# Two broadcast rows by DMA through DRAM, and the subtraction of q's maximum on GpSimd, in a fused attention and graph kernel

## What is computed

```python
# layer 0, per batch: x (C=256, N=512)
q, k = wq @ x, wk @ x
scores = leaky_relu(q[None, :] + k[:, None], 0.01)      # N x N
att = softmax(scores, axis=-1)
out0 = relu(adj @ (x @ att.T) + bm[:, None])
h = layernorm(x + out0)
# layer 1, per batch: h (N=256, D=512)
z_l, z_g, v = h @ W_lang.T, h @ W_grav.T, h @ W_V.T
zn = z_l / max(norm(z_l), 1e-8)
A_l = max(zn @ zn.T, 0) * not_eye * mask                # mask = adj
A_g = exp(-dist2(z_g) / (2 sigma^2)) * not_eye * mask
K = w * A_l / rowsum(A_l) + (1 - w) * A_g / rowsum(A_g)
y = layernorm(h + (K @ v) @ W_O.T)
```

## Time and profile before

| | us |
|---|---|
| median of 3 runs | 1203.2 |
| lowest, highest | 1196.25, 1203.94 |
| the profiled execution, its span | 1203.0 |

### The profile page before, as it was taken

How to read it: one execution, slowest core, us unless ns; L and a number is a source line. 1 busy time by engine, 2 the same in 40 slices (tenths; PEclk the granted TensorE clock), 3 DMA queues, 4 the chain that set the end, 5 groups by cost and what they waited for, 6 DMA issues and landing times.

```text
span 1203.0 us, 21861 instructions
## 1 busy us (share of the span) xinstructions
PE 1080.8 (90%) x7296; PEld 712.7 (59%) x7296; DVE 946.9 (79%) x2678; ACT 657.9 (55%) x1299; POOL 333.8 (28%) x316
## 2 busy tenths in 40 slices
PE   7757989989998999999899998989989998998996
PEld 4344756756575675657567565656756565575663
DVE  4557878978787897878789787878978787897867
ACT  2435656565565656556565655656565564756431
POOL 0231414224051422405142240414233041423200
PEclk9979999999999998999999999999999999999998
DMA  7002002020020202002020200102020020201000
GB/s 262 0 1 71 1 1 106 2 105 0 19 85 0 105 0 105 0 21 84 0 105 0 105 0 30 75 0 105 0 105 0 34 71 0 105 0 70 1 35 36
DMA packets 22763, 55.40 MB, mean 46 GB/s; under 512 B 1744, under 2 KB 2256, under 8 KB 20688
## 3 DMA queue, kind: packets, MB, share of 16 engines
q1 hardware_dynamic: 22736, 55.06, 12.5%
HBM read 21.50 MB, written 16.78 MB: 32 GB/s over the span
## 4 chain that ended last, share of the span: by engine, by line
PE 32%; issue 28%; DVE 21%; POOL 9%; ACT 7%; DMA 1%; DVEq 1%; POOLq 0%; SPq 0%; ACTq 0%
PE bank L225 9%; PE bank L227 9%; PE bank L226 9%; POOL att_lo L1103 7%; DVE a_g L926 4%; DVE o_stat L748 2%; PE bank L463 2%; PE bank L413 2%; ACT a_g L535 2%; DVE att L826 2%; DVE a_l L960 2%; DVE a_l L914 1%; PE bank L352 1%; DVE t_lo L799 1%; ACT agg_t L583 1%
## 5 line engine op out<-in xcount | busy, mean ns | idle before, releaser
L1103 POOL TENSOR_TENSOR att_lo<-att,att_hi 128x512 f16<-128x512 f32 x128 | 157.2, 1236 | 170.8 <-ACT att_hi L516 155.0
L826 DVE SCALAR_TENSOR_TENSOR att<-a_row,u_col,vb 128x512 f32<-128x512 f32 x128 | 130.0, 1035 | 41.2 <-POOL att_lo L1103 39.6
L225 PE MATMUL bank<-xw_hi,att_hi 128*128 128x257 f16 x512 | 141.6, 276 | 16.8 <-DVE ug_lo L704 15.2
L225 PE MATMUL bank<-ht_hi,z_hi 128*128 128x256 f16 x512 | 139.7, 273 | 3.8 <-DVE b_row L818 3.0
L227 PE MATMUL bank<-xw_hi,att_lo 128*128 128x257 f16 x512 | 140.5, 274 | 0.0
L226 PE MATMUL bank<-xw_lo,att_hi 128*128 128x257 f16 x512 | 140.3, 274 | 0.0
L226 PE MATMUL bank<-ht_lo,z_hi 128*128 128x256 f16 x512 | 139.6, 273 | 0.0
L227 PE MATMUL bank<-ht_hi,z_lo 128*128 128x256 f16 x512 | 139.6, 273 | 0.0
L604 ACT ACTIVATE xw_hi<-bank 128x256 f16<-128x256 f32 x128 | 49.1, 385 | 108.4 <-PE bank L227 108.4
L516 ACT ACTIVATE att_hi<-att 128x512 f16<-128x512 f32 x128 | 79.6, 622 | 52.3 <-DVE att L826 52.3
L583 ACT ACTIVATE agg_t<-bank,den_inv 128x256 f32<-128x256 f32 x128 | 59.0, 474 | 88.6 <-DVE den_inv L773 88.5
(11 more groups left out here) (177 smaller groups left out, 2807.9 us busy)
## 6 DMA issues: line engine op xcount, KB each, us to landing
x_in<-in_x SPq DMA_DIRECT2D x16, 1024.0 KB, 5.3
x_res<-x_in SPq DMA_DIRECT2D x16, 1024.0 KB, 4.8
out_y<-o SPq DMA_DIRECT2D x32, 512.0 KB, 3.1
agg_t<-in_wl SPq DMA_DIRECT2D x4, 256.0 KB, 3.5
y<-in_wg SPq DMA_DIRECT2D x1, 1024.0 KB, 10.2
o<-in_wv SPq DMA_DIRECT2D x1, 1024.0 KB, 12.3
h<-in_woT SPq DMA_DIRECT2D x1, 1024.0 KB, 14.5
att<-in_adjT SPq DMA_DIRECT2D x1, 256.0 KB, 4.0
```

Source lines behind the costliest of these rows:

```text
L225: pe.matmul(dst, ah, bh, start=(i == 0 and first), stop=False, skip_group_check=skip)
L826: dve.scalar_tensor_tensor(out=att[:, g % 2, :], in0=a_row[:, j, :], scalar=u_col[:, j, n:n + 1], in1=vb[:, g % 2, :], op0=ALU.mult, op1=A ...
L1103: pool.tensor_tensor(att_lo[:, n[0], n[1], :], att[:, g % 2, :], att_hi[:, n[0], n[1], :], ALU.subtract).then_inc(s["att_lo_done"], 1)
```

## The change

It has three parts.

- **k.** `k_hi`, `k_lo`, `dk_hi`, `dk_lo`, `k_rows` and their semaphores go. SP stores column k of `qk` (128 partitions x 8 words) into a DRAM tensor `k_line` when the last `xw_lo` is written, waits for the store, and loads the line of 1,024 words into `k_row` on all 128 partitions (4 KB each). `t_rows` reads `k_row` in SBUF.
- **r.** `diag_r` and `norm_rows` go. SP waits for `r_l`, stores it (128 x 4 words) into `r_line`, waits, and loads 512 words into `r_row` on all partitions (2 KB each). The masked product on VectorE reads `r_row` and `mask`, both in SBUF. Waits of TensorE for the banks that held the two rows go.
- **q_rel.** GpSimd subtracts q_max itself, in one instruction of 128x8, behind the all-reduce; VectorE's two subtractions and its wait for `q_max` at that place go.

In SP's order the r transfers stand behind the load of x_in, the k transfers behind them, and the output stores last. The edit of the list of semaphore names is left out here, and most lines around the changed ones.

```diff
--- before.py
+++ after.py
@@ -105,8 +105,8 @@
         q_cols = qk[:, :, 0].rearrange("p (j n) -> p j n", j=2)
-        k_hi, k_lo = sb("k_hi", [2 * NC], F16), sb("k_lo", [2 * NC])
-        dk_hi, dk_lo = sb("dk_hi", [2 * NC, P], F16), sb("dk_lo", [2 * NC, P], F16)
+        k_row = sb("k_row", [2, N])
+        k_line = nc.dram_tensor("k_line", (2 * NC, P), F32, kind="Internal").ap()
         u_col, v_col = sb("u_col", [2, NC]), sb("v_col", [2, NC])
@@ -126,7 +126,8 @@
         neg_g = sb("neg_g", [4])
-        diag_r = sb("diag_r", [4, P])
+        r_row = sb("r_row", [2, O])
+        r_line = nc.dram_tensor("r_line", (4, P), F32, kind="Internal").ap()
         a_l, a_g = sb("a_l", [2, OC, O]), sb("a_g", [2, OC, O])
@@ -207,6 +208,24 @@
                     sp.dma_start(mask[:], adj.rearrange("(c p) m -> p c m", p=P)).then_inc(s["mask_loaded"], 16)
+                if l1:
+                    wait(sp, s["mr_done"], 2 * p)
+                    sp.wait_ge(s["r_l_done"], p + 1)
+                    sp.dma_start(r_line.rearrange("k p -> p k"), r_l[:],
+                                 allow_slow_non_contiguous=True).then_inc(s["r_stored"], 16)
+                    sp.wait_ge(s["r_stored"], 16 * (p + 1))
+                    sp.dma_start(r_row[:].rearrange("p j m -> p (j m)"),
+                                 r_line.rearrange("k p -> (k p)").partition_broadcast(P))\
+                        .then_inc(s["r_loaded"], 16)
+                if new:
+                    sp.wait_ge(s["xw_lo_done"], 8 * r + 8)
+                    sp.dma_start(k_line.rearrange("n p -> p n"), qk[:, :, 1],
+                                 allow_slow_non_contiguous=True).then_inc(s["k_stored"], 16)
+                    sp.wait_ge(s["k_stored"], 16 * (r + 1))
+                    wait(sp, s["t_done"], 2 * r)
+                    sp.dma_start(k_row[:].rearrange("p j n -> p (j n)"),
+                                 k_line.rearrange("n p -> (n p)").partition_broadcast(P))\
+                        .then_inc(s["k_loaded"], 16)
                 if l1:
@@ -252,7 +271,7 @@
                 pe.wait_ge(s["wo_loaded"], 16)
-                pe.wait_ge(s["t_done"], 2)
+                pe.wait_ge(s["xw_lo_done"], 8)
                 for d in rows:
@@ -265,20 +284,7 @@
-                def k_rows():
-
-                    pe.wait_ge(s["dk_hi_done"], q + 1)
-                    pe.wait_ge(s["dk_lo_done"], q + 1)
-                    for j, b in ((0, 7), (1, 4)):
-                        pe.wait_ge(s["xw_lo_done"], 8 * q + 8)
-                        n = slice(j * NC, (j + 1) * NC)
-                        pe.matmul(bank[b][:], ones16[:], dk_hi[:, n, :].rearrange("p a n -> p (a n)"),
-                                  start=True, stop=False)
-                        pe.matmul(bank[b][:], ones16[:], dk_lo[:, n, :].rearrange("p a n -> p (a n)"),
-                                  start=False, stop=True).then_inc(s["k_mm"], 1)
-
                 if l0 and not l1:
-                    k_rows()
                     gram(1, between=lambda: fuse_weights((0,)))
@@ -298,16 +304,12 @@
                                                  for d in range(block_e + 1)]).then_inc(s["z_mm"], 1)
-                        if l0 and g == (3 if up else 1):
-                            k_rows()
-
                     def t_product(k):
                         kind, j = k // 2, k % 2
                         pe.wait_ge(s["z_lo_done"], 8 * p + 4 * kind + 4)
                         if k == 0:
                             if l0:
-                                pe.wait_ge(s["t_done"], 2 * q + 2)
                                 pe.wait_ge(s["xw_lo_done"], 8 * q + 8)
@@ -346,12 +348,6 @@
-                    def norm_rows():
-
-                        pe.wait_ge(s["diag_r_done"], p + 1)
-                        pe.matmul(bank[3][:], ones[:], diag_r[:].rearrange("p a n -> p (a n)"),
-                                  start=True, stop=True).then_inc(s["r_mm"], 1)
-
                     v_product(0)
@@ -362,7 +358,6 @@
                     else:
-                        norm_rows()
                         v_product(1)
@@ -377,8 +372,6 @@
                             pe.wait_ge(s["v_lo_done"], 4 * p + k + 1)
-                        if l1 and k == 3:
-                            pe.wait_ge(s["mr_done"], 2 * p + 2)
                         if at(p, -1) and k == 3:
@@ -386,8 +379,6 @@
                                                           for n in range(NC)]).then_inc(s["ot_mm"], 1)
-                        if l1 and k == 0:
-                            norm_rows()
@@ -615,11 +606,6 @@
                 if new:
-                    act.wait_ge(s["k_lo_done"], r + 1)
-                    wait(act, s["k_mm"], 2 * r)
-                    for n in range(2 * NC):
-                        last = act.activation(dk_lo[:, n, :], ident16[:], ACT.Copy, scale=k_lo[:, n:n + 1])
-                    last.then_inc(s["dk_lo_done"], 1)
                     act.wait_ge(s["q_rel_done"], r + 1)
@@ -811,11 +797,11 @@
                 def t_rows():
-                    for j, b in ((0, 7), (1, 4)):
-
-                        dve.wait_ge(s["k_mm"], 2 * q + j + 1)
-                        dve.tensor_scalar(a_row[:, j, :], bank[b][:], q_max[:, j:j + 1], 0.0, ALU.add, ALU.min)
-                        dve.tensor_scalar(b_row[:, j, :], bank[b][:], q_max[:, j:j + 1], 0.0, ALU.add, ALU.max)\
+                    dve.wait_ge(s["k_loaded"], 16 * (q + 1))
+                    dve.wait_ge(s["q_max_done"], q + 1)
+                    for j in range(2):
+                        dve.tensor_scalar(a_row[:, j, :], k_row[:, j, :], q_max[:, j:j + 1], 0.0, ALU.add, ALU.min)
+                        dve.tensor_scalar(b_row[:, j, :], k_row[:, j, :], q_max[:, j:j + 1], 0.0, ALU.add, ALU.max)\
                            .then_inc(s["t_done"], 1)
@@ -882,10 +868,6 @@
                     v_lo_tile(0)
-                    dve.wait_ge(s["r_l_done"], p + 1)
-                    for k in range(4):
-                        last = dve.tensor_scalar(diag_r[:, k, :], ident[:], r_l[:, k:k + 1], None, ALU.mult)
-                    last.then_inc(s["diag_r_done"], 1)
                     if l0:
@@ -900,9 +882,9 @@
-                        dve.wait_ge(s["r_mm"], p + 1)
+                        dve.wait_ge(s["r_loaded"], 16 * (p + 1))
                         for c in range(OC):
-                            last = dve.tensor_tensor(a_l[:, j, c, :], halves[3][:, j, :], mask[:, c, :], ALU.mult)
+                            last = dve.tensor_tensor(a_l[:, j, c, :], r_row[:, j, :], mask[:, c, :], ALU.mult)
                         last.then_inc(s["mr_done"], 1)
@@ -995,6 +977,7 @@
                         dve.wait_ge(s["uv_done"], r)
+                        dve.wait_ge(s["k_stored"], 16 * r)
                     dve.wait_ge(s["xr_loaded"], 16 * (q + 1))
@@ -1042,6 +1025,7 @@
                     wait(dve, s["uv_done"], r)
+                    wait(dve, s["k_stored"], 16 * r)
                     for k in range(4, 8) if x_first else range(4):
@@ -1055,17 +1039,6 @@
                     dve.tensor_reduce(q_part[:], q_cols, AX.X, ALU.max).then_inc(s["q_part_done"], 1)
-                    dve.tensor_copy(k_hi[:], qk[:, :, 1]).then_inc(s["k_hi_done"], 1)
-                    dve.wait_ge(s["k_hi_done"], r + 1)
-                    dve.tensor_tensor(k_lo[:], qk[:, :, 1], k_hi[:], ALU.subtract).then_inc(s["k_lo_done"], 1)
-                    for n in range(2 * NC):
-                        last = dve.tensor_scalar(dk_hi[:, n, :], ident16[:], k_hi[:, n:n + 1], None, ALU.mult)
-                    last.then_inc(s["dk_hi_done"], 1)
-                    dve.wait_ge(s["q_max_done"], r + 1)
-                    wait(dve, s["uv_done"], r)
-                    for j in range(2):
-                        last = dve.tensor_scalar(q_rel[:, j, :], q_cols[:, j, :], q_max[:, j:j + 1], None, ALU.subtract)
-                    last.then_inc(s["q_rel_done"], 1)
@@ -1132,6 +1105,10 @@
                     pool.partition_all_reduce(q_max[:], q_part[:], P, RMAX).then_inc(s["q_max_done"], 1)
+                    pool.wait_ge(s["q_max_done"], r + 1)
+                    wait(pool, s["uv_done"], r)
+                    pool.tensor_tensor(q_rel[:], q_cols, q_max[:].unsqueeze(2).broadcast_to([P, 2, NC]), ALU.subtract)\
+                        .then_inc(s["q_rel_done"], 1)
                 if at(p, -2):
```

More of the change, by code:

```diff
@@ L158, in build @@
             wvo_hi_done wm_lo_done wqk_lo_done wvo_lo_done wvo_mm knobs_done tiny_done x_hi_done
-            x_lo_done wx_mm xw_hi_done xw_lo_done k_mm k_hi_done k_lo_done dk_hi_done dk_lo_done
+            x_lo_done wx_mm xw_hi_done xw_lo_done k_stored k_loaded
             q_part_done q_max_done q_rel_done uv_done t_done ab_done vb_done att_done att_hi_done
@@ L162, in build @@
             y_var_done y_rstd_done h_done ht_mm ht_hi_done ht_lo_done z_mm z_hi_done z_lo_done t_mm
```

(4 more changed lines are left out.)

## The result

| | us |
|---|---|
| before, median of 4 runs | 1200.53 |
| after, median of 4 runs | 1529.26 (1528.74 to 1532.75) |
| ratio after to before, 95% interval | 1.273 (1.270 to 1.277) |
| the profiled execution of after, its span | 1527.0 |

A forecast was written before the change was run, and what follows sets the result against it. TensorE, 90% busy, was taken to stall 2.55 us a step on q_rel behind GpSimd's q_max. 1203.0 + 106.2 (switch) + 8.5 (setup) + 52.5 (r row) - 6 (k row) = 1364 us; range 1300 to 1412.

The forecast's parts named there:

- The way back before q_rel, 7.28 a step: GpSimd's program switch from all-reduce to elementwise work, put before q_rel: u_col +7.08 us a step, 15 times, +106.2.
- The k row, "hidden by the stall itself", -6: k's two DMA transfers finish before t_rows wants them; faster t_rows gives -0.4 us a step, -6 in all.
- The way in: GpSimd's program switch into the all-reduce, idle before q_max: 5.86 us now, no change per step counted.
- The store, taken at 3.9 us: r's store of 512 single words to DRAM, sized from a 3.3 us load; with the 3.5 load, r lands at 704.4.
- rival 2: Single-word stores are slow, some 4 us beyond the range's end: r at 711 costs 7.5 a step, 1424 us; chance 0.12.
- The slow clock behind the r row, 0.5: TensorE's low clock after stopping before output product 4: 0.5 us added per step, part of it hiding behind VectorE.
- The lock between x_lo and the masked product: Masked products with two SBUF inputs stand still during GpSimd's x_lo, starting at 707.1, 4.9 later; first instance over 0.42 us.
- the forecast's 3.5 a step: Cost of the r row by DMA: +3.5 us a step, ends +1.4 and +5.5, 15 steps, +52.5.
- The clock at the large stall, 0: TensorE's extra slow-clock time after the longer wait for q_rel: counted 0, at most +0.8 a step, +12.
- t_rows from SBUF: VectorE's t_rows reads SBUF instead of PSUM: 542 ns against 743, -0.4 us a step, ends 0 and -0.8.
- The setup, 8.5: In the setup, q_rel between two all-reduces adds switches both ways: +8.5 us, up to 10.5; att_lo starts near 53.
- The sum by step: Per step: 7.08 for the switch before q_rel, 3.5 for the r row, less 0.4 for faster t_rows.

The follow-up runs named there:

- only_qrel: The kernel before with only q_rel's subtraction moved to GpSimd (t_rows then waits for q_max), both rows still by matmul: 1311.24 us, ratio 1.092.
- only_k: The kernel before with only the k row by DMA, stored in single words; q_rel on VectorE, r by matmul: 1263.95 us, ratio 1.053.
- store_early: The kernel before plus the word-wise store of k, issued where after issues it and read by nobody: 1248.01 us, ratio 1.039.
- only_r: The kernel before with only the r row by DMA, stored as 512 single words: 1334.35 us, ratio 1.111.
- only_r_compact: The kernel before with only the r row by DMA, stored as it lies in 128 pieces, read through a strided view: 1253.37 us, ratio 1.042.
- after_compact: The kernel after with both stores in 128 pieces as the words lie (VectorE copies k first), rows read strided: 1358.74 us, ratio 1.132.
- before_ahead: The kernel before with GpSimd's loop written out and the small addition turn_q ahead of q_max removed: 1132.63 us, ratio 0.943.

## Why the prediction was wrong in size

- **The way back before q_rel, 7.28 a step: right alone, 9.80 in the step shown.** only_qrel has 7.0 each time and 110 us in all, against 114.7 forecast. In after it is 9.07 on average, with the end of the store and the load of k beside it. MODIFY_POOL_CONFIG stands at q_rel's line, as named:

```profile
L1110 POOLq MODIFY_POOL_CONFIG  x32: 82/83/83, 33.4 to 1385.9; - x32
```

- **The k row, "hidden by the stall itself", -6: this step failed.** As a wait it was right: t_rows waits for it only once, in the setup. What was not asked is what the transfers do to others. The way in, which the sum left at 5.86, was 9.56 in the step shown (on average 9.24, where before had 6.12); only_k costs 63 us, store_early, with nothing but the store, 46. The traffic fell into the one stretch of the step in which the whole kernel stood behind GpSimd.
- **The store, taken at 3.9 us, was the mis-sized term of r.** I scaled a load of 128 single words (3.3) to 512. Issue of the store to issue of the load was 8.98 (median 9.1), and the load took 4.9, not 3.5. Moved back by v_lo 2, the products start at 700.68 + 10.40 = 711.1 in the times of before. That is the place of rival 2, for which the text had 7.5 a step. What the sum below leaves for r and t_rows together is 8.1, and only_r alone pays 8.9 for each of 15 steps. So the mechanism behind that price was right and its size nearly; the chance of 0.12 was too low: "Nothing in the profile speaks for it or against" was true of a trace that had no such row, and a bound worked out from loads is no bound for stores.
- **The slow clock behind the r row, 0.5, was too small.** TensorE now stands still for 7.84 us before output product 4 and goes on at 806.85 with a low clock, in a part of the step that in before ran at 1.00. The clock is 0.50 up to 808.50; the window behind it (the third number from the end is the clock), and one of before:

```profile
808.50:812.00 3.50, 3.50 (x20) 2.49 (x18) 3.45 (x19) 0.95 (x2) 0.00 (x0) 0.54 0.00 0
```

```profile
701.00:716.00 15.00, 14.50 (x120) 11.65 (x118) 12.77 (x48) 9.41 (x18) 4.79 (x3) 1.00 0.00 0
```

  From 806.85 to 812.00 TensorE is busy for 5.15 us at about half speed, which is 2.6 us of work, by an estimate from these rows. How much of it hides behind VectorE no run shows.

- **The lock between x_lo and the masked product was not reached in after**, as the row lands after x_lo ends, so the first product is no longer than 0.42 us and that sign failed. It is there in only_r_compact, near the forecast's 3.5 a step (3.4, with 0.8 of it from the strided view).
- **The clock at the large stall, 0: right.** After 16.69 us of idleness TensorE's granted clock was low for about as long as before (0.50 until past 767.0, so some 3.3 us, as in the earlier trace rows):

```profile
764.00:767.70 3.70, 3.45 (x9) 1.28 (x10) 3.67 (x12) 0.94 (x2) 0.00 (x0) 0.55 0.00 0
```

- **t_rows from SBUF: right, a little better.** 478 ns, against 743 in PSUM and the 542 taken.
- **The setup, 8.5:** att_lo starts at 58.39, where 53 was named: 13.9 later than before, as both switches are longer here too.

The sum by step: forecast 7.08 + 3.5 - 0.4 = 10.2. The step shown is longer than most (turn_q at 742.30 and again at 833.43, 91.1 us), so take the mean: from the second q_max to the last it is 89.97 us in after (125.99 to 1385.53, 14 steps) and 69.92 in before (108.86 to 1087.78), 20.05 more. The 9.9 above the forecast are 3.1 for the way in (9.24 less 6.12), 1.8 for the way back (9.07 less 7.28), and 5.0 as the remainder, for r with its clock and t_rows (8.1 where 3.5 - 0.4 was forecast). 15 times 9.9 and 5.4 in the setup is 153, which with 1364 makes 1517, for a span of 1527.0; the 10 us left lie in the first and the last steps and were not followed up.

**What stays open.** Through what the traffic reaches GpSimd's switch is argued, not shown, and so is what makes neighbouring single words slow. The Trainium skill, GPSIMD Engine Reference, Terminology, says that ModifyPoolConfig loads a library by DMA at run time, which would put the code on the same engines behind the words. The trace has no packets that follow the 32 switches (its instruction queues count 11 to 15 packets in every kernel). How large the stretch of DRAM is within which neighbours hold each other up was not tried either, only 4 and 64 bytes apart.

## What to carry to other kernels

A transfer that nobody waits for is not free: ask what else is on its way in that stretch, and above all whether GpSimd is changing its program there. Do not store a column of single words so that neighbours in DRAM come from different partitions; store the words of a partition as they lie, and let the reader take the strided view. And when a switch of program stands behind a wait for data, look for the instruction in front of it that keeps it there: taking away one small addition was worth 68 us.

## What was not expected of the hardware

- 256 neighbouring single words, 8.2 us to landing; 1,024 of them, 10.1; 1,024 words 64 bytes apart, 2.7; 1,024 pieces of 32 bytes, 2.4; 128 pieces of 32 or 16 bytes, 1.4. The smallest load of before was at 3.3.
- GpSimd's way into the all-reduce takes 5.9 to 6.1 us alone, 5.9 beside the 512 KB load (after_compact) and 8.8 beside the word-wise store; the way back takes 7.0 to 7.3 alone, 9.1 beside the end of the store and the 512 KB load behind it, 11.4 beside the store, 14.1 beside store and load.
- Four products with both inputs in SBUF take 2.2 us alone and 5.8 beside GpSimd's x_lo (only_r_compact).
- The switch needs no data and starts ahead of the semaphore wait of the instruction it is for (before_ahead), so a wait of 9.5 us for q_part hides it whole.
